# Softmax probabilities turned in 32x32 blocks by VectorE and moved by SBUF transfers, in place of TensorE transposes

## The reference, cut to what matters

```python
h = concat([ctx, layernorm(x)], axis=1)              # 256 keys a batch
q, k, v = layernorm(x) @ Wq, h @ Wk, h @ Wv          # 32, 4 and 4 heads of 128
attn = softmax(q @ k.T / sqrt(128))                  # a head: 128 x 256
x = x + (attn @ v) @ Wo
r = softmax(layernorm(x) @ gate_w.T)                 # 8 experts
x = x + ((layernorm(x) * (r @ in_scale)) @ sign(W).T) * (r @ out_scale) + bias
```

## Time and profile before

| | us |
|---|---|
| runs, median of three | 738.65 |
| profiled execution, span | 737.0 |
| PE busy | 725.1 |
| DVE busy | 400.4 |
| ACT busy | 363.7 |
| POOL busy | 266.6 |

### The profile page before, as it was taken

One profiled execution on the slowest core, in us unless ns is written; L12 is line 12 of the kernel. 1 busy time (PEld: TensorE's weight loads), 2 busy tenths in 40 slices (PEclk: granted clock), 3 DMA queues, 4 the chain that ended last, 5 costly groups with the idle time before them and its releaser, 6 DMA issues.

```text
span 737.0 us, 11712 instructions
## 1 busy us (share of the span) xinstructions
PE 725.1 (98%) x3880; PEld 617.3 (84%) x3880; DVE 400.4 (54%) x742; ACT 363.7 (49%) x945; POOL 266.6 (36%) x316
## 2 busy tenths in 40 slices
PE   7999999999999999999999999999999999999996
PEld 5888888888888888888888888888888888888874
DVE  4552233664366436643664366436643664768876
ACT  3343324663466346634663466346634663465642
POOL 4243003441344134413441344134413441445554
PEclk9999999999999999999999999999999999999999
DMA  9566459110112320101223201012242010000001
GB/s 322 206 228 235 172 214 314 42 55 5 58 59 86 95 104 0 57 0 57 63 79 103 96 0 57 0 57 72 74 124 74 1 58 1 1 0 16 15 30 58
DMA packets 28418, 60.59 MB, mean 82 GB/s; under 512 B 2088, under 2 KB 2088, under 8 KB 27360
## 3 DMA queue, kind: packets, MB, share of 16 engines
q1 hardware_dynamic: 28384, 60.15, 24.0%
HBM read 41.27 MB, written 18.87 MB: 82 GB/s over the span
## 4 chain that ended last, share of the span: by engine, by line
PE 95%; DVE 2%; issue 1%; POOL 1%; DMA 1%; ACT 0%; SPq 0%; DVEq 0%; ACTq 0%; POOLq 0%
PE bank L947 48%; PE bank L1076 23%; PE bank L1059 12%; PE bank L1042 7%; PE bank L1158 1%; PE bank L1113 1%; DMA raw_a<-in_L_xattn_Wv 1%; PE bank L956 1%; DVE wq_pair L647 0%; PE bank L964 0%; PE bank L1105 0%; DVE stats L650 0%; PE bank L1128 0%; DVE acc L743 0%; PE bank L1091 0%
## 5 line engine op out<-in xcount | busy, mean ns | idle before, releaser
L351 POOL TENSOR_TENSOR prob<-prob,rsum 128x512 f32<-128x512 f32 x128 | 133.6, 1046 | 218.0 <-DVE rsum L731 218.0
L1076 PE MATMUL bank<-wo_pair,oT 128*128 128x512 f32 x768 | 203.5, 403 | 0.0
L947 PE MATMUL bank<-xT,wq_pair 128*128 128x512 f32 x768 | 184.0, 392 | 0.0
L947 PEld LDWEIGHTS bank<-xT,wq_pair 128*128 128x128 f32 x768 | 142.0, 188 | 28.8
L1076 PEld LDWEIGHTS bank<-wo_pair,oT 128*128 128x128 f32 x768 | 136.9, 188 | 24.8
L496 ACT ACTIVATE prob<-bank,nmax 128x256 f32<-128x256 f32 x256 | 118.6, 470 | 24.8 <-DVE nmax L725 24.8
L947 PEld LDWEIGHTS bank<-kg,qT 128*128 128x128 f32 x768 | 108.0, 189 | 9.5
L947 PE MATMUL bank<-kg,qT 128*128 128x256 f32 x768 | 112.7, 282 | 0.0
L313 POOL TENSOR_TENSOR wo_pair<-raw_b,wo_pair 128x512 fp32r<-128x512 f32 x32 | 41.0, 1312 | 189.2 <-ACT wo_pair L417 189.2
L417 ACT ACTIVATE pT<-bank 128x512 fp32r<-128x512 f32 x128 | 75.5, 597 | 59.2 <-PE bank L1042 59.2
L718 DVE SCALAR_TENSOR_TENSOR qT<-bank,qT 128x512 fp32r<-128x512 f32 x64 | 44.2, 691 | 107.8 <-ACT qT L487 107.8
(11 more groups left out here) (85 smaller groups left out, 576.7 us busy)
## 6 DMA issues: line engine op xcount, KB each, us to landing
v_park<-v_stage SPq DMA_DIRECT2D x8, 1024.0 KB, 4.3
raw_a<-in_L_xattn_Wq SPq DMA_DIRECT2D x8, 1024.0 KB, 6.8
raw_b<-in_L_xattn_Wo SPq DMA_DIRECT2D x8, 1024.0 KB, 5.4
k_park<-k_stage SPq DMA_DIRECT2D x8, 1024.0 KB, 3.9
kg<-k_park SPq DMA_DIRECT2D x32, 256.0 KB, 3.0
vg<-v_park SPq DMA_DIRECT2D x32, 256.0 KB, 3.2
craw<-in_ctx SPq DMA_DIRECT2D x8, 256.0 KB, 5.8
acc<-in_x SPq DMA_DIRECT2D x8, 256.0 KB, 5.9
```

The costliest lines, as they stand in the source:

```text
L351: nc.gpsimd.tensor_tensor(prob[:, p], prob[:, p], rsum[:, p].unsqueeze(2).to_broadcast([P, 2, KEYS]), ALU.mult).then_inc(prob_ready[p], 1)
L947: last = nc.tensor.matmul(dst, left(a, c), right(b, c), start=(n == 0), stop=(n == 3 * chunks - 1))
L1076: last = nc.tensor.matmul(wo_bank[:, :], oT[:, s, h, :], wo_pair[:, w, h, :], start=((s, w) == TERMS[0] and h == 0), stop=((s, w) == TERMS ...
```

## The change

The probabilities are no longer turned by TensorE. `turn` on VectorE transposes every 32x32 block of a head pair in place of its row and column (one 128x512 instruction from SBUF to SBUF, two a step) into `p_turned`. `move_p` on SP then issues sixteen transfers a step, each from 32 partitions to 32 others, 1 KB a partition, into `p_low`. ScalarE rounds that 128x1024 block into `p_high` (`p_half`), GpSimd subtracts in place (`p_rest`), and `attend` reads both. Keys are stored in a permuted order that fits. The turned buffers are double, so scores run three steps ahead of `attend`, also over the border of two quads, and each step holds one q unit. The rest of Wo goes to VectorE (`wo_rest`, four at a quad's step 0), that of Wq stays on GpSimd (`wq_rest`, in four of a quad's eight steps). `project_out` runs in its own step, behind `attend`, scores and q unit. The final quad follows the same `step`, with the FFN parts put between. The SP loop over groups is unrolled. The core of the diff:

```diff
-            pT = sb(att, "pT", [P, 2, KC, QH, T], f32r)
+            p_turned = sb(att, "p_turned", [P, 2, NB, QH, 32])
+            p_high = sb(att, "p_high", [P, 2, QB, KC, QH * 32], f32r)
+            p_low = sb(att, "p_low", [P, 2, QB, KC, QH * 32], f32r)
             oT = sb(att, "oT", [P, 2, QH, T], f32r)
...
+            def move_p(g, qd, t, first=False):
+                for p in range(2):
+                    sp.wait_ge(turned[p], steps(g, qd, t + 1))
+                if not first:
+                    sp.wait_ge(av_ready, steps(g, qd, t - 1))
+                for j in range(QB):
+                    for i in range(QB):
+                        sp.dma_start(
+                            words(p_low[32 * j:32 * (j + 1), t % 2, i]).rearrange("r c q -> r (c q)"),
+                            p_turned[32 * i:32 * (i + 1), t % 2, KC * j:KC * (j + 1)].rearrange(
+                                "r k h q -> r (k h q)")).then_inc(p_in[t % 2], 16)
...
+            def step(g, qd, t, last):
+                final = last and qd == QUADS - 1
+                if not (final and t + 2 >= B):
+                    move_p(*step_after(g, qd, t, 2))
+                if t == 1 and not final:
+                    sp.wait_ge(wo_lo, count(g, QH, qd, QH))
+                    load_wo(*quad_after(g, qd, 1))
+                if t == 3 and not final:
+                    ng, nqd = quad_after(g, qd, 1)
+                    sp.wait_ge(wq_lo, count(ng, QH, nqd, QH))
+                    if last:
+                        sp.dma_start(raw_a[:, :, :], ffn_w.rearrange("(c p) n -> p c n", p=P)
+                                     ).then_inc(ffn_in, 16)
+                    else:
+                        load_wq(*quad_after(g, qd, 2))
+                if qd == QUADS - 1 and not last:
+                    for p in range(2):
+                        sp.wait_ge(s_ready[p], steps(g, qd, t + 1))
+                    sp.wait_ge(av_ready, steps(g, qd, t + 1))
+                    load_kv(g + 1, t)
...
+            def p_rest(g, qd, t):
+                pool.wait_ge(p_hi, steps(g, qd, t + 1))
+                part = p_low[:, t % 2].rearrange("p i c q -> p (i c q)")
+                nc.gpsimd.tensor_tensor(part, part.bitcast(fp32),
+                                        p_high[:, t % 2].rearrange("p i c q -> p (i c q)"),
+                                        ALU.subtract).then_inc(p_lo, 1)
+            def wq_rest(g, qd, h):
+                cols = head_cols(h)
+                pool.wait_ge(wq_hi, count(g, QH, qd, h + 1))
+                nc.gpsimd.tensor_tensor(wq_pair[:, LO, :, cols], raw_a[:, :, cols],
+                                        wq_pair[:, HI, :, cols], ALU.subtract).then_inc(wq_lo, 1)
+            def step(g, qd, t, last):
+                final = last and qd == QUADS - 1
+                if not (final and t + 2 >= B):
+                    normalise(*step_after(g, qd, t, 2), 1)
+                if not (final and t + 1 >= B):
+                    p_rest(*step_after(g, qd, t, 1))
+                if t == B - 1 and not last:
+                    wq_rest(*quad_after(g, qd, 2), 0)
+                if t < QH - 1 and not final:
+                    wq_rest(*quad_after(g, qd, 1), t + 1)
+                if final and t >= 1:
+                    make_rstd(B + t - 1)
+                if final and t >= 2:
                     bias_add(t - 2)
+                if not (final and t + LEAD >= B):
+                    normalise(*step_after(g, qd, t, LEAD), 0)
+                if final and t >= 3:
                     ffn_add(t - 3)
...
+            def p_half(g, qd, t):
+                act.wait_ge(p_in[t % 2], 16 * QB * QB * pairs(g, qd, t))
+                copy(p_high[:, t % 2].rearrange("p i c q -> p (i c q)"),
+                     p_low[:, t % 2].bitcast(fp32).rearrange("p i c q -> p (i c q)")).then_inc(p_hi, 1)
...
+            def wo_half(g, qd, h):
+                if h == 0:
+                    act.wait_ge(wo_in, 16 * count(g, 1, qd, 1))
+                if h < QH - 1:
+                    act.wait_ge(wo_free, count(g, QH - 1, qd, h + 1))
+                else:
+                    act.wait_ge(wo_ready, steps(g, qd, 0))
+                split_hi(wo_pair, raw_b, h, wo_hi)
...
+            def step(g, qd, t, last):
+                final, b = last and qd == QUADS - 1, t - 2
+                ahead = None if final and t + LEAD >= B else step_after(g, qd, t, LEAD)
+                if not (final and t + 1 >= B):
+                    p_half(*step_after(g, qd, t, 1))
+                if t == 0:
+                    wo_half(g, qd, 0)
+                    wo_half(g, qd, 1)
+                o_half(g, qd, t)
+                if t == 0:
+                    wo_half(g, qd, 2)
+                    wo_half(g, qd, 3)
+                if final and b >= 1:
+                    z_half(b - 1)
+                if ahead:
+                    exps(*ahead, 0)
+                if t == B - 1 and not last:
+                    wq_half(*quad_after(g, qd, 2), 0)
+                if t < QH - 1 and not final:
+                    wq_half(*quad_after(g, qd, 1), t + 1)
                 if t == 0:
                     q_half(g, qd, UNITS - 1)
+                elif not final:
+                    q_half(*quad_after(g, qd, 1), t - 1)
+                if final and t == 1:
+                    for c in range(HC):
+                        sgn_copy(c)
+                if final and b >= 0:
                     yt_copy(b)
+                if ahead:
+                    exps(*ahead, 1)
+                if final and b >= 0:
+                    gate_exp(b)
                     routet_copy(b)
                     oscale_copy(b)
...
+            def turn(g, qd, t, p, first=False):
+                dve.wait_ge(prob_ready[p], steps(g, qd, t + 1))
+                if not first:
+                    dve.wait_ge(p_in[t % 2], 16 * QB * QB * (pairs(g, qd, t) - 1))
+                nc.vector.transpose(
+                    p_turned[:, t % 2, :, 2 * p:2 * p + 2, :].rearrange("p k h q -> p h k q"),
+                    prob[:, p].rearrange("p h (k e) -> p h k e", e=32)).then_inc(turned[p], 1)
+            def wo_rest(g, qd, h):
+                dve.wait_ge(wo_hi, count(g, QH, qd, h + 1))
+                subtract(wo_pair[:, LO, h, :], raw_b[:, h, :], wo_pair[:, HI, h, :]).then_inc(wo_lo, 1)
...
+            def step(g, qd, t, last):
+                final, b = last and qd == QUADS - 1, t - 2
+                ahead = None if final and t + LEAD >= B else step_after(g, qd, t, LEAD)
+                if t == 0:
+                    wo_rest(g, qd, 0)
+                if not (final and t + 2 >= B):
+                    turn(*step_after(g, qd, t, 2), 1)
+                if t == 0:
+                    wo_rest(g, qd, 1)
+                if ahead:
+                    row_max(*ahead, 0)
+                o_rest(g, qd, t)
+                if t == 0:
+                    wo_rest(g, qd, 2)
+                    wo_rest(g, qd, 3)
+                if final and b >= 1:
+                    z_rest(b - 1)
+                if final and b >= 0:
+                    ffn_norm(b)
+                if ahead:
+                    row_recip(*ahead, 0)
+                    turn(*ahead, 0)
                 if t == 0:
                     q_rest(g, qd, UNITS - 1)
+                elif not final:
+                    q_rest(*quad_after(g, qd, 1), t - 1)
+                if last and not final and t >= B - HC:
+                    sgn(t - (B - HC))
+                if final and b >= 1:
+                    ffn_scale(b - 1)
+                if ahead:
+                    row_max(*ahead, 1)
+                if final and b >= 0:
+                    gate_max(b)
+                if ahead:
+                    row_recip(*ahead, 1)
+                if final and b >= 0:
+                    gate_route(b)
+                accumulate(g, qd, t)
+                if final:
+                    ffn_stats(t)
+                if final and b >= 0:
                     z_make(b)
...
-            def transposes(g, qd, t, p):
-                pe.wait_ge(prob_ready[p], steps(g, qd, t + 1))
-                pe.wait_ge(pt_lo[p], steps(g, qd, t))
-                for kc in range(KC):
-                    for j in range(2):
-                        at = (2 * kc + j) * T
-                        last = nc.tensor.transpose(t_bank[p][:, at:at + T],
-                                                   prob[:, p, j, kc * P:(kc + 1) * P], ident[:, :])
-                last.then_inc(pt_ready[p], 1)
...
-                pe.wait_ge(pt_hi[1], steps(g, qd, t + 1))
-                pe.wait_ge(pt_hi[0], steps(g, qd, t + 1))
-                for vs, ps in ((HI, HI), (LO, HI), (HI, LO)):
-                    if ps == LO:
-                        pe.wait_ge(pt_lo[0], steps(g, qd, t + 1))
-                        pe.wait_ge(pt_lo[1], steps(g, qd, t + 1))
+                pe.wait_ge(p_hi, steps(g, qd, t + 1))
```

(40 more changed lines are left out.)

479 lines of the change are left out of this document (152 added, 327 removed).

## The result

Four runs of the changed kernel took 951.15 to 956.09 us, median 952.12; the kernel before took 738.83 beside them. The ratio is 1.29, 95% interval 1.2872 to 1.2928. The forecast was 774.7, range 728 to 817: the direction was right, the size was not, and the time lies far outside the range. The profiled execution, the slowest of the four, has a span of 953.9 us.

The account below looks back on a forecast made before the run. Closed loops through in-order engines were to bound the kernel, mainly the two-step loop through SP's transfers: 132.1 + 7.5 + 7 x 74.0 + 93.4 + 22 = 773.0 us of span, plus 1.65, gives 774.7 us, range 728 to 817.

Parts of the forecast that it names:

- PE's own step: PE's work per step without the transposes: 9.17 less 0.81, so 8.36 us, a quad 66.9.
- landing: Time until a step's sixteenth transfer on SP has landed: 2.0 us, bounds 1.6 and 2.4.
- the place where PE waits: PE idle ahead of `project_out`, released by `o_rest` on DVE, some 0.8 us a step.
- the chain of the gate in the final quad: From `attend` through POOL's list, `turn` and exponentials to the gate and `project_out`: 15.0 us in steps 2 to 4.
- Rival 3: `turn` on DVE takes 1.2 us: 4.4 us more a quad, 806 us in all; chance 0.09.
- SP's issues: Sixteen transfers a step on SP, 0.375 us apart, the sixteenth 5.6 us after the first; SP's sum 6.0 us.
- rival 2: SP's issues are 0.475 us apart: 6.0 us more a quad, 817 us in all; chance 0.13.
- loop B: Two-step loop from `turn` through SP's transfers, ACT, POOL and DVE back to `turn`: 18.2 us mean, 9.1 a step.
- Wo on VectorE: Four `wo_rest` a quad on DVE wait while POOL works: 0 to 4 us a quad, taken as 1.3.
- loop A: One-step loop from pair 1's exponentials through POOL and DVE back: 8.06 us, 9.37 with a `wq_rest`, mean 8.7.
- Final quad and tail: Final quad 93.4 us plus tail 22: 115.4 against 91.2 before, 24 more.
- The clock: PE's gaps lower its clock; not priced, held unlikely; chance 0.03 together with something else.

Follow-up runs that it names:

- four_moves: Changed kernel with four transfers a step of 128 rows by 1 KB in place of sixteen, same bytes, blocks in wrong places; 802.3 us.
- gate_first: four_moves with the gate's work put first in the final quad on POOL, ACT and DVE; 791.6 us.
- wo_first: four_moves with, in step 0 of each quad, all `wo_half` ahead of `p_half` on ACT and all `wo_rest` ahead of `turn` on DVE; 797.5 us.
- wq_last: four_moves with POOL taking `wq_rest` behind the normalisation of pair 0, not ahead of it; 766.5 us.
- all_orders: four_moves with the three orders of wo_first, gate_first and wq_last together; 740.4 us.
- keep_busy: Changed kernel with eight extra matmuls a step ahead of `project_out` in all but the last quad; 969.8 us.

## Why the prediction was wrong, point by point

**What was right.** The direction, and the kind of reason: closed loops through engines that work in order. (That no engine is full by its sum held for all but SP, as the next point says.) PE's own step (8.28 measured in four_moves, 8.36 predicted), `turn` (0.71 for 0.65), `p_half` (1.06 for 1.05), `p_rest` (2.37 for 2.62), landing (1.8 for 2.0), the start (8.4 for 7.5 us), the place where PE waits, and the chain of the gate in the final quad: gate_first takes PE's wait for it from 3.82 to 0.27 us. Rival 3 is out: `turn` is one pass, not two.

**The term that failed: SP's issues.** I took 0.375 us with bounds 0.34 and 0.475. All rows there have HBM at one end. I asked how partitions and bytes move the price, and chose by that; the run shows that neither does and that the end that I never saw in the trace, SBUF on both sides, costs 0.63. The bounds came from the nearest rows, and the nearest rows were of another kind, without a word on that; rival 2 was this mechanism at three quarters of its price. In place of 5.6 us stand 9.5 up to the sixteenth: 3.8 us more a loop, 1.9 a step, 15 a quad. With it SP's own sum is 10.1 us a step, 11 with loads, above PE's 8.3, where I had it at 6.0; and loop B, with the prediction's other terms as they stand, is 22.1 us for two steps, 11.0 a step. The steps behind step 0 measured 11.1.

**Wo on VectorE.** Taken as 1.3 us a quad, measured near 6: over seven quads step 0 takes 16.9 us and the others 11.1 in the change, 14.2 and 8.7 in four_moves. The lock behind `p_rest` is 1.8 us in the change and 2.1 in four_moves, once a quad. That is nearer to the whole instruction of 2.6 that the prediction set beside it than to the 1.0 of the earlier trace rows, which was beside passes half as long. But wo_first shows that the lock isn't the core of it: 1.6 us of it went, and step 0 fell by 1.1. That the four passes on two engines lie in loop A fits wq_last and all_orders, where step 0 falls once `wq_rest` is out of that loop.

**The sum again.** Quad: 74.0, plus 15.2 for the issues, plus 4.5 for Wo (5.8 less the 1.3 in the sum), 93.7; measured 94.9. Over seven quads the miss is 146 of the 177 us, of which these two terms give 138. Final quad and tail: 149.1 against 115.4. Steps 2 to 4 took 17.3 to 19.1 instead of 15.0, in part because `project_out`'s second half runs partly at the lower clock behind its wait; 12 us go with the issues (149.1 against 137.4 in four_moves); and step 7 with the tail took 39.5, not 32.4. The start adds 0.9, and the median lies 1.8 under the span, not 1.65 above.

**What made up for what.** four_moves has next to none of the issue term, and its quads take 75.0 us, near the 74.0 predicted. That is no proof of loop B: with four issues it is 13.5 us for two steps and doesn't bind. The 75.0 are PE-dense steps, one to three of 9.6 us as loop A gives with a `wq_rest` (9.37 predicted), and Wo's 6 us. So that nearness is luck.

**The clock.** Held at 0.03 and left out of the sum. Its mean fell to 0.902, and 25 of 57 `project_out` in the change take 4.1 to 5.3 us in place of 3.0. keep_busy, with a mean of 0.946 and 9 of them, is no faster, so the clock isn't the main cause; what it adds apart from the waits is not shown.

## What to carry over

Price an operation by a row of the same kind, and ask what makes the kind: for a transfer, where both its ends are. If no such row exists, the bound must go beyond the nearest rows, and a term that is taken sixteen times a step deserves that first. When an engine in order gets long instructions (issues, or a double pass), look at what stands behind it in its list: the same four issues a step made the kernel 94 us slower or faster, by their place.
